# Last stage of a graph kernel: node groups of two tiles, two expert steps a slot, five slots behind the edges

## What is computed

```python
# L1 gnn: h = layernorm(x) @ weight, summed over 100,000 edges, sorted by dst
msgs = edge_val[:, None] * h[edge_src]
agg = jax.ops.segment_sum(msgs, edge_dst, num_segments=6250)
x = x + agg + bias
# L1 ffn, on layernorm(x): 32 experts, one chosen for each node
idx = jnp.argmax(xf @ router_w.T + router_b, axis=-1)
h = relu(einsum('nd,ndh->nh', xf, W1[idx]) + b1[idx])       # 256 -> 64
x = x + relu(einsum('nh,nhd->nd', h, W2[idx]) + b2[idx])    # 64 -> 256
```

## Time and profile before

| | us |
|---|---|
| median of 3 runs | 3277.88 |
| lowest, highest | 3269.11, 3279.42 |
| the profiled execution's own time | 3279.42 |
| its span, first to last instruction | 3279.4 |
| last stage with edges, slots 17 to 26 | 60.4 |
| slots 27 to 195 | 1059.9 |
| after the last edges | 83.5 |

### The profile page before, as it was taken

One profiled execution on the slowest core, in us unless ns is written; L12 is line 12 of the kernel. 1 busy time (PEld: TensorE's weight loads), 2 busy tenths in 40 slices (PEclk: granted clock), 3 DMA queues, 4 the chain that ended last, 5 costly groups with the idle time before them and its releaser, 6 DMA issues. The chain is left out here.

```text
span 3279.4 us, 51092 instructions
## 1 busy us (share of the span) xinstructions
PE 2782.1 (85%) x17781; PEld 2480.7 (76%) x17781; DVE 2084.8 (64%) x3782; ACT 2041.7 (62%) x4125; POOL 2023.7 (62%) x1692
## 2 busy tenths in 40 slices
PE   6899837799999999999999944788888988888889
PEld 6789726688888888888888834677777777777778
DVE  8689654577676777677766535556555655656652
ACT  4377456687888788777876525545455555555551
POOL 0355467676677677776773028776677777766750
PEclk9999957799999999999999975689898998989989
DMA  2133452223233323232331023233333333323320
GB/s 67 5 85 74 111 165 87 73 89 94 84 92 94 94 86 96 87 95 84 91 95 58 14 82 114 87 96 92 94 89 97 97 103 97 94 85 92 99 74 14
DMA packets 159242, 280.89 MB, mean 86 GB/s; under 512 B 42474, under 2 KB 107778, under 8 KB 158722
## 3 DMA queue, kind: packets, MB, share of 16 engines
q0 software_dynamic: 87808, 207.48, 22.3%
q1 hardware_dynamic: 70884, 68.48, 6.7%
q10 hardware_dynamic: 288, 1.61, 0.1%
HBM read 240.67 MB, written 36.77 MB: 85 GB/s over the span
## 5 line engine op out<-in xcount | busy, mean ns | idle before, releaser
L1310 POOL DMA_INDIRECT f_got<-h_tab,list_cols x784 | 952.8, 1215 | 390.1 <-issue 235.9
L1953 POOL DMA_INDIRECT n_got<-h_tab,edge_cols x784 | 894.4, 1141 | 333.9 <-issue 226.9
L2069 PE MATMUL bank<-n_mhi,n_hot 128*128 128x256 f32 x1168 | 339.1, 318 | 155.6 <-DMA n_got<-h_tab,edge_cols 99.3
L2016 ACT ACTIVATE n_hrh<-bank 128x512 fp32r<-128x512 f32 (+1 forms) x208 | 118.9, 572 | 560.4 <-remote 275.9
L1580 DVE TENSOR_TENSOR f_hlo<-edge_cols,f_hhi 128x1024 fp32r<-128x1024 f32 (+1 forms) x208 | 241.6, 1161 | 331.9 <-ACT f_hhi L1389 266.8
L1384 ACT ACTIVATE edge_cols<-bank,f_shf,f_scl 128x512 f32<-128x512 f32 (+1 forms) x416 | 296.3, 745 | 169.3 <-PE bank L1301 114.8
L1466 PE MATMUL bank<-f_mhi,f_hot 128*128 128x256 f32 x1168 | 330.7, 314 | 64.9 <-DVE f_mlo L1574 55.6
L2069 PEld LDWEIGHTS bank<-n_mhi,n_hot 128*128 128x128 f32 x1168 | 246.0, 211 | 184.2 <-DMA n_got<-h_tab,edge_cols 108.8
L1997 ACT ACTIVATE n_got<-n_got,edge_cols 128x256 f32<-128x256 f32 x784 | 333.1, 500 | 79.1 <-DMA n_got<-h_tab,edge_cols 78.8
L1362 ACT ACTIVATE f_got<-f_got,list_cols 128x256 f32<-128x256 f32 x784 | 332.5, 496 | 44.3 <-DMA f_got<-h_tab,list_cols 44.1
L2070 PE MATMUL bank<-n_mlo,n_hot 128*128 128x256 f32 x1168 | 324.0, 305 | 28.5 <-issue 28.2
(11 more groups left out here) (318 smaller groups left out, 7599.5 us busy)
## 6 DMA issues: line engine op xcount, KB each, us to landing
f_got<-h_tab,list_cols POOLq DMA_INDIRECT x784
n_got<-h_tab,edge_cols POOLq DMA_INDIRECT x784
n_rows<-acc_tab SPq DMA_DIRECT2D x12, 512.0 KB
out_rows<-n_rows SPq DMA_DIRECT2D x12, 512.0 KB
edge_cols<-in_w SPq DMA_DIRECT2D x16, 256.0 KB
acc<-in_x SPq DMA_DIRECT2D x4, 896.0 KB, 7.2
h_tab<-hbuf SPq DMA_DIRECT2D x7, 512.0 KB
acc_tab<-base SPq DMA_DIRECT2D x7, 512.0 KB
```

The source lines that it names most:

```text
L1310: nc.gpsimd.indirect_dma_start(got[:, s % RING0, u, :], None, h_tab[0], bass.IndirectOffsetOnAxis(gidx0[:, s * U + u:s * U + u + 1], 0), b ...
L1953: nc.gpsimd.indirect_dma_start(got[:, s % RING, u, :], None, h_tab[1], bass.IndirectOffsetOnAxis(gidx[:, s * U + u:s * U + u + 1], 0), bou ...
L2069: nc.tensor.matmul(tile_bank(t), lhs, mhi[:, s % 3, u, :], start=begins, stop=False)
```

## The change

Groups of two tiles in place of four, so 25 groups of 16 steps. Two steps in each slot, with 256 columns each. The lags of turn, logits, choice and mask are one or two slots shorter, and the first step stands in slot 9. The rings of relu's parts have four buffers in place of two, output sums alternate between banks 4 and 5 by group, and DVE makes the lower halves ahead of the next slot's messages. Core of the diff:

```diff
+GS4 = 2
+NG4 = -(-NTILES // GS4)
+WIDTHS4 = (1,) + (GS4,) * (NG4 - 1)
+ROW_RING = 4
+STEP_RING = 4
...
-            rows = sb4("n1_rows", [P, 3 * GS, D])
+            rows = sb4("n1_rows", [P, ROW_RING * GS4, D])
...
-            hrh = sb4("n1_hrh", [P, 2, W4], F32R)
-            hrl = sb4("n1_hrl", [P, 2, W4], F32R)
+            hrh = sb4("n1_hrh", [P, STEP_RING, W2], F32R)
+            hrl = sb4("n1_hrl", [P, STEP_RING, W2], F32R)
...
-            AT_SUM, AT_NORM, AT_TURN, AT_LOG, AT_PICK, AT_MASK, AT_FFN = 1, 2, 3, 4, 5, 6, 7
+            AT_SUM, AT_NORM, AT_TURN, AT_LOG, AT_PICK, AT_MASK, AT_FFN = 1, 2, 2, 3, 4, 4, 5
...
-            FIRST = WIDTHS[0] * U + AT_FFN
-            SLOTS = FIRST + NG * PAIRS + OUTPUT + 1
+            PACE4 = 2
+            FIRST = WIDTHS4[0] * U + AT_FFN
+            SLOTS = FIRST + NG4 * PAIRS // PACE4 + OUTPUT + 1
...
-            def out_tile(k):
-                return bank[4 + k // 2][:, (k % 2) * D:(k % 2) * D + D]
+            def out_tile(g, k):
+                return bank[4 + g % 2][:, k * D:k * D + D]
...
-                        if g:
-                            pe.wait_ge(s_y, FIRST_TILE[g])
+                        if g >= 2:
+                            pe.wait_ge(s_y, FIRST_TILE4[g - 1])
...
                 for s in range(SLOTS):
                     if s < EGROUPS:
                         edges(s)
-                    n = step_at(s - OUTPUT)
-                    if n is not None:
+                    for n in steps_at(s - OUTPUT):
                         outputs(n)
-                    n = step_at(s)
-                    if n is not None:
-                        if n == 0:
-                            pe.wait_ge(s_selc, 7)
-                            pe.wait_ge(s_wsplit, 6)
+                    for n in steps_at(s):
                         hidden(n)
...
                 for s in range(SLOTS):
-                    n = step_at(s - OUTPUT - 1)
...
+                    for n in steps_at(s - RELU):
+                        w = width(n // PAIRS) * P
+                        dve.wait_ge(s_r, n + 1)
+                        if n >= STEP_RING:
+                            dve.wait_ge(s_used, n - STEP_RING + 1)
+                        nc.vector.scalar_tensor_tensor(hrl[:, n % STEP_RING, 0:w], bank[n % 2][:, 0:w], 0.0,
...
+                    for n in steps_at(s - OUTPUT - 1):
+                        if n % PAIRS == PAIRS - 1:
...
                     if s + 1 < EGROUPS:
                         messages(s + 1)
-                    n = step_at(s - RELU)
```

More of the change, by code:

```diff
@@ L1900, in tile_at, with steps_at @@
                 return t if r == 0 and 0 <= t < NTILES else None
[L1902 to L1904 removed]
+            def steps_at(s):
+                at = (s - FIRST) * PACE4
+                return range(at, at + PACE4) if 0 <= at < NG4 * PAIRS else ()
             def width(g):
[L1907 removed]
+                return WIDTHS4[g]
             def node_tiles(s):
@@ L1960, in tile_rows @@
                 def tile_rows(table, g):
-                    return table[FIRST_TILE[g] * P:FIRST_TILE[g + 1] * P, :].rearrange("(k p) d -> p k d", p=P)
+                    return table[FIRST_TILE4[g] * P:FIRST_TILE4[g + 1] * P, :].rearrange("(k p) d -> p k d", p=P)
                 def group_rows(g):
-                    return rows[:, g % 3 * GS:g % 3 * GS + width(g), :]
-                for g in range(NG + 2):
-                    if g < NG:
+                    return rows[:, g % ROW_RING * GS4:g % ROW_RING * GS4 + width(g), :]
+                for g in range(NG4 + ROW_RING - 1):
+                    if g < NG4:
                         if g:
                             wait_apart(sp, s_accin, g * 16)
-                        if g >= 3:
-                            wait_apart(sp, s_st, (g - 2) * 16)
+                        if g >= ROW_RING:
+                            wait_apart(sp, s_st, (g - ROW_RING + 1) * 16)
                         sp.dma_start(group_rows(g), tile_rows(acc_tab[1][0], g)).then_inc(s_accin, 16)
@@ L1984, in _ @@
                             sp.dma_start(PIECES[i][2], PIECES[i][3]).then_inc(landed, 16)
[L1985 to L1988, removed]
+                    n = g - ROW_RING + 1
+                    if n >= 0:
+                        wait_apart(sp, s_y, FIRST_TILE4[n + 1])
+                        sp.dma_start(tile_rows(out, n), group_rows(n)).then_inc(s_st, 16)
+                sp.wait_ge(s_st, 16 * NG4)
             @block.scalar
@@ L2176, in _ @@
                 for s in range(SLOTS):
-                    n = step_at(s - OUTPUT - 1)
[L2178 to L2183, removed]
+                    for n in steps_at(s - RELU):
+                        w = width(n // PAIRS) * P
+                        dve.wait_ge(s_r, n + 1)
+                        if n >= STEP_RING:
+                            dve.wait_ge(s_used, n - STEP_RING + 1)
+                        nc.vector.scalar_tensor_tensor(hrl[:, n % STEP_RING, 0:w], bank[n % 2][:, 0:w], 0.0,
+                                                       hrh[:, n % STEP_RING, 0:w].bitcast(F32),
+                                                       ALU.max, ALU.subtract).then_inc(s_rl, 1)
+                    for n in steps_at(s - OUTPUT - 1):
+                        if n % PAIRS == PAIRS - 1:
+                            g = n // PAIRS
+                            dve.wait_ge(s_used, n + 1)
+                            for k in range(width(g)):
+                                at = row(FIRST_TILE4[g] + k)
+                                nc.vector.scalar_tensor_tensor(at, out_tile(g, k), 0.0, at, ALU.max, ALU.add).then_inc(s_y, 1)
                     if s + 1 < EGROUPS:
                         messages(s + 1)
[L2186 to L2194, removed]
                     t = tile_at(s, AT_SUM)
```

45 lines of the change are left out of this document (24 added, 21 removed).

## The result

The changed kernel takes 3312.18 us (median of 7 runs, 3301.55 to 3335.11) where the kernel before took 3277.88 beside it. The ratio is 1.0112, with a 95% interval of 1.0084 to 1.0140. The forecast was 3264, its range ended at 3302, and the sign was wrong. The profiled execution took 3318.89 us with a span of 3317.2.

What follows compares the result with a forecast made beforehand. POOL's gathers were taken to set the pace between the edges, and PE alone the tail. Terms of -30.8, -0.7, -0.9, +2.7, 0, +9, +13 and -6 sum to -13.7 us against 3279.4, forecast 3264; range 3240 to 3302.

Steps and rivals of the forecast that it cites:

- Terms 1 and 2: After the last edge matmul PE has fewer columns left, -30.8 us; at the very end, sums -0.7 and store -0.9 us.
- term 7: Outputs get two banks, so PE's wait for the sums of the group before goes: -6 us, between 0 and -9.
- Term 3: Work leaving the tail goes between the edges, PE's total unchanged; slots 17 to 26 take 6.31 us each: +2.7 us.
- The rule against it: Skill page's spacing of load and matmul pairs on PE: 1,344 more loads add 34 us, sum +20; not followed.
- Term 6: On DVE lower halves now precede messages, so mlo releases POOL's ring buffer 2.0 us later: +13 us, at most 54.
- rival A: DVE's loop delays mlo and holds POOL: 20 us of Term 5, 45 of Term 6, 3307 us; chance 0.24.
- Term 5: PE's transposes move into the slot of DVE's normalisation and wait some 0.6 us: +9 us, between 0 and 29.
- Term 4: ACT's relus and DVE's lower halves become two pieces each: +0.16 us a slot on each engine, 0 by itself.
- What bounds the kernel: POOL, working or issuing 89% of the long part, sets the pace; PE falls behind in bursts and alone sets the tail.
- rival C: PE's 256-column hidden matmuls cannot start before weight loads of 0.19 us end: 188 us more, 3452 us; chance 0.02.

## Why the prediction was wrong

The changed kernel's +1.12% (37 us) is made up, by ratios and the profiled tails, of four parts: the tail -31; the pieces on PE +28.5; DVE's order +23; the work moved among the edges +10 (a third of 31). Their sum is +30, and the intervals of the parts are wider than the 7 that are missing. The pieces were measured in the kernel before and the other two in the changed kernel; that the parts add up is assumed.

- **Terms 1 and 2, the tail and the very end**, were right: 31.2 us together for 32.4. The end gave 1.4 for 1.6 (the two sums 0.65, the store 0.8), so some 30 were the tail's for 30.8. The wait before L2112 for the sums (term 7) went as said, and 36.6 us of it came back where the outputs had one bank again, but its 6 us can't be told in any run.
- **Term 3, "PE's work in sum is unchanged"**, is the step that failed first. The columns are unchanged; the time of the stage is not, when they come in more pieces. I read 0.118 us for 256 columns at an undisturbed spot and used it for a stretch of which the mean clock, 0.91, already said that it is disturbed. The pieces stood at nothing in the sum and measured +28.5. The moved work itself stood at +2.7, covered by POOL's pace; by the run with the later steps it is some +10, with an interval that holds the 2.7 too. Slots 17 to 26 took 6.6 us each, not 6.31.
- **The rule against it.** The case showed 28.5 us for the pieces, 18 to 39. The Trainium skill (page TensorE: Matmul & The Clock Gate, Back-to-back issue gap) gave 34 by its figures, an estimate; its sum of +20 would have been 3298. Its 25 ns are for matmuls of 128 columns and were taken over to 256. The measurement agrees with the size, and not with the way: in the tail, where PE alone sets the end, a piece costs 6 ns and not 25. That the sizes meet is luck as far as the runs show. The sentence of the prediction that "the row for 256 columns disagrees, so the sum goes by the row" was right on the spacing and wrong on the cost.
- **Term 6, the order**, was mis-sized, 13 for 23, though the interval of the 23, 9 to 36, doesn't exclude 13. The direction was as described, and in the kernel before the order raised POOL's wait for mlo from 133.9 to 206.9 us on one chip. In the changed kernel that wait went to 179 us where I had 115 and rival A over 130, but PE's pieces raise it too, so it doesn't measure the order. I took a quarter of the bound because slack should outlast a burst. The runs paid 23 and, in the kernel before, 44 of the bound of 54.
- **Term 5, the turn**, was bounded at 29 us by 0.6 us in 49 slots, and the idle time came to 64 us in 36 in the long stretch. Yet taking it away gave back nothing that a median shows, some 7 us against my 9. The bound was wrong and the term held: in the kernel before, 46 us of the same idle time cost nothing that could be measured.
- **Term 4** was right at nothing, by itself. **What bounds the kernel** was put too simply. POOL works or issues in 89% of the time, but it does not cover PE: nothing but PE's matmuls was changed in the run with the pieces, and it cost 28.5 us, 19 us of which show as POOL's wait for mlo. So PE's work is on the path as well. That it gets there in the bursts is a reading of the waits that no run tested by itself.

Rival A came within some 5 us of the result, by luck, with half its cause. It put 65 us on the loop through DVE; the loop has 23, the turn next to nothing, and the rest belongs to rival C's subject, the pieces, at a sixth of its price.

Not settled: why pieces cost 20 us more among the edges than in the tail. Whether each piece is one more place to be stopped at, or the mean clock falls first, no run separated. Over all executions on that chip the clock of the whole span was 0.891 on average with the pieces (8) and 0.899 in the kernel before (20); but the changed kernel with the old order had 0.900 (10) where the kernel before had 0.898 (21), and was slower all the same. Nor is it known what the disturbances are. A kernel with wide groups first and narrow ones only at the end, which might keep the short tail without most of the pieces, was not tried.

## What to carry to other kernels

Price a piece of work by its mean over the stretch into which it goes, stalls and low clock included, not by an undisturbed spot: halving the hidden matmuls cost 28.5 us here, more than three times what the quiet stretch would make of the same pieces, 8 us. Don't rest a reading on one profile's idle time: POOL's wait for mlo was 138.7 and 197.4 us in two profiles of the same kernel, on two chips, while the ratios agreed. On an engine that serves two loops, put first what refills the ring that sets the pace, and behind it what waits for a late engine; the reverse cost 0.7% and 1.35% here. And before a new idle time in a profile is blamed, take it away: the largest new wait of PE in this one was worth some 7 us, which the interval doesn't tell from nothing.

## What the runs showed of the hardware

A 512-column matmul of these operands made as two of 256 costs 6 ns more for each added piece in a quiet stretch and 28.5 us / 1,344 = 21 ns on average over the whole stage, 14 to 29 by the interval. In the quiet stretch these matmuls start 230 ns apart with 512 columns and 118 ns with 256. The granted clock of slots 27 to 195, between the levels of 1.2 and 2.4 GHz, was 0.87 on average with the pieces and 0.90 without, in one profiled execution of each on one chip. The kernel before itself differed by 1.3% between chips (3277 to 3319 us), more than the change is worth.
